# One pipeline for the first update, the second normalisation and the score tables of a two-layer graph network

## The reference, cut to what matters

```
h = max(layernorm(x), 0)
# layer 0: messages by edge type, summed by destination, then a GRU update
m = segment_sum((A[type] @ h)[src], dst);  x = x + GRU0(m, h)
h = max(layernorm(x), 0)                   # the second normalisation
# layer 1: attention over the edges of each source
score = w2 . relu(W_src h[src] + W_attr attr + W_dst h[dst] + b)
msg = segment_sum(softmax_by_src(score) * lin(h[dst]), src);  x = x + GRU1(h, msg)
```

## Time and profile before

| what | us |
|---|---|
| median of three runs (lowest, highest) | 7402.01 (7397.92, 7403.58) |
| time of the profiled execution | 7396.92 |
| its span | 7395.1 |
| layer-0 update, first turn to last add | 2476.0 to 2595.2 |
| second normalisation | 2595.2 to 2634.7 |
| score tables, first turn to last split | 2636.2 to 2810.0 |

### The profile page before, as it was taken

How to read it: one execution, slowest core, us unless ns; L and a number is a source line. 1 busy time by engine, 2 the same in 40 slices (tenths; PEclk the granted TensorE clock), 3 DMA queues, 4 the chain that set the end, 5 groups by cost and what they waited for, 6 DMA issues and landing times.

```text
span 7395.1 us, 188373 instructions
## 1 busy us (share of the span) xinstructions
PE 5695.5 (77%) x35043; PEld 4674.5 (63%) x35044; DVE 4531.8 (61%) x20027; ACT 2116.9 (29%) x6104; POOL 4910.9 (66%) x10199
## 2 busy tenths in 40 slices
PE   4555778888655747888788898886888888888885
PEld 2355555555555536777677787775677677767773
DVE  3466777777333663333333333333999999999997
ACT  3111100000000212222222222222555555555553
POOL 0377777777777105777777777776677777777771
PEclk8755555555555767656765656656888988898889
DMA  6233333333333123333333333333333333333332
GB/s 211 80 57 58 59 56 58 58 58 58 59 58 58 25 97 97 107 109 106 103 102 102 102 102 102 102 102 127 94 94 94 93 94 94 94 93 94 94 91 71
DMA packets 1128085, 648.93 MB, mean 88 GB/s; under 512 B 782034, under 2 KB 1031684, under 8 KB 1127045
## 3 DMA queue, kind: packets, MB, share of 16 engines
q1 hardware_dynamic: 766708, 357.79, 19.9%
q0 software_dynamic: 137728, 233.30, 11.2%
q10 hardware_dynamic: 223584, 57.12, 3.3%
HBM read 360.62 MB, written 311.42 MB: 91 GB/s over the span
## 4 chain that ended last, share of the span: by engine, by line
PE 26%; issue 21%; POOL 17%; DMA 15%; DVE 14%; ACT 4%; DVEq 1%; POOLq 1%; ACTq 1%; SPq 0%
DMA wide<-msg_table,ring 10%; PE banks L1278 9%; POOL wide L746 7%; PE banks L1280 6%; POOL rows_by_src L770 3%; PE banks L1325 3%; DVE h L1809 2%; DVE ring L1820 2%; DMA rows_by_src<-ring 2%; PE banks L1279 2%; DVE h L1814 2%; PE banks L1266 1%; PE banks L1190 1%; PE banks L1316 1%; ACT ring L981 1%
## 5 line engine op out<-in xcount | busy, mean ns | idle before, releaser
L770 POOL DMA_INDIRECT rows_by_src<-ring x1760 | 1784.6, 1014 | 564.7 <-issue 492.8
L746 POOL DMA_INDIRECT wide<-msg_table,ring x1664 | 1619.0, 973 | 769.3 <-issue 467.2
L1278 PE MATMUL banks<-wide,ring 128*128 x3520 | 1253.1, 454 | 238.6 <-ACT ring L974 154.0
L1278 PEld LDWEIGHTS banks<-wide,ring 128*128 128x128 f32 x3520 | 828.2, 290 | 321.0 <-issue 319.2
L1280 PE MATMUL banks<-h,ring 128*128 x3520 | 973.5, 374 | 0.0
L1280 PEld LDWEIGHTS banks<-h,ring 128*128 128x128 f32 x3520 | 845.6, 295 | 125.4
L981 ACT COPY ring<-banks 128x416 f32<-128x416 f32 x880 | 402.2, 509 | 1635.7 <-PE banks L1280 1635.7
L1190 PE MATMUL banks<-wide,ring 128*128 x3520 | 810.9, 411 | 65.9 <-DVE ring L1668 61.4
L1190 PEld LDWEIGHTS banks<-wide,ring 128*128 128x128 f32 x3520 | 780.0, 322 | 127.3 <-issue 123.5
L1777 DVE COPY ring<-ring 128x4 f32<-128x4 f32 x440 | 80.4, 183 | 1230.9 <-DMA rows_by_src<-ring 1230.8
L1155 PE MATMUL banks<-ident,ring 128*128 128x128 f32 x1248 | 424.2, 469 | 532.3 <-ACT ring L917 273.8
(11 more groups left out here) (315 smaller groups left out, 10848.6 us busy)
## 6 DMA issues: line engine op xcount, KB each, us to landing
h<-rows_by_src SPq DMA_DIRECT2D x1776, 105.0 KB, 2.0
ring<-attr_turned SPq DMA_DIRECT2D x440, 128.0 KB, 2.4
attr_turned<-ring ACTq DMA_DIRECT2D x416, 96.0 KB
rows_by_src<-ring POOLq DMA_INDIRECT x1760
wide<-msg_table,ring POOLq DMA_INDIRECT x1664
msg_table<-ring SPq DMA_DIRECT2D x100, 256.0 KB, 2.0
ring<-attr_by_dst SPq DMA_DIRECT2D x208, 64.0 KB
attr_turned<-ring ACTq DMA_DIRECT2D x208, 64.0 KB
```

The lines of the kernel that those rows point to most:

```text
L746: g.indirect_dma_start(out=A_g[:, b * GV + u, :], out_offset=None, in_=table[:, :], in_offset=bass.IndirectOffsetOnAxis(ap=A_idx[:, s, u:u ...
L770: g.indirect_dma_start(out=rows_d[:, :], out_offset=bass.IndirectOffsetOnAxis(ap=B_pos[:, s, u:u + 1], axis=0), in_=B_row[:, s, u, :], in_ ...
L1278: mm(b[:, 0:H1], B_DT[:, t, u, :], q_tab[:, w, :].rearrange("p a k -> p (a k)"), start=True, stop=False)
```

## The change

The three stages become one written-out sequence of 63 slots (`G_SLOTS` = 50 + 11 + 2) on PE, ACT, DVE, and 66 on SP. Slot k of the sequence holds, in each engine's order:

- PE: turn pair k; gate products of pair k-1; turn `h` of pair k-11 (into one bank, 4, straight from `h`, no GpSimd copy); one product of 288 columns per window for pair k-12 (banks 5 and 6, one buffer).
- ACT: copy of pair k; candidate tanh of pair k-2; gate tanh of pair k-1; in every fifth slot a `Square` of ten windows of `h`; copy to `P_hT` of pair k-11; copies of both products of pair k-12, to `q_tab` and to `P_raw` in SBUF. The copies of the edge ids (`recs1`) stand in slot 51.
- DVE: mix of pair k-1; candidate of pair k; a step of the normalisation of ten windows; the bf16 split of pair k-13, out of `P_raw`.
- SP: load of pair k's half of `h0m`; store of `P_hT` of pair k-14; store of the bf16 parts of pair k-16. The 3,200 KB stores of `xs` and `h`, the padding rows and the loads for `rows` come after the last of these.

The normalisation goes by groups of ten windows (five pairs), the steps at slots 5g+6 (sum, deviation), 5g+7 (`Square` on ACT), 5g+8 (sum of squares, then an inverse square root by shift, subtraction and three Newton rounds) and 5g+9 (one instruction for maximum and scale). ScalarE's `Sqrt` of this normalisation is gone. `normalise`, still used for the first one, loses its two multiplications by 1/64 and does maximum and scale in one instruction. VectorE's memsets of the padding buffers come after the whole sequence. The semaphores of the layer-1 update are shared with those of layer 0.

```diff
+G_GROUP = 5
+N_GROUPS = NW // 2 // G_GROUP
+G_NORM = (G_GROUP + 1, G_GROUP + 2, G_GROUP + 3, G_GROUP + 4)
+G_LAG = 2 * G_GROUP + 1
+G_SLOTS = NW // 2 + G_LAG + 2
+G_STORE = G_LAG + 5
...
@@ SP @@
+            for k in range(NW // 2 + G_STORE):
+                if k < NW // 2:
+                    if k >= H_SLOTS:
+                        sp.wait_ge(g_mm, k - H_SLOTS + 1)
+                    sp.dma_start(h0m[0:HID, k % H_SLOTS, :, :]..., h0T_d[:, k * 2 * P:(k + 1) * 2 * P])...
+                j = k - G_LAG - 3
+                if 0 <= j < NW // 2:
+                    sp.wait_ge(p_Tc, j + 1)
+                    sp.dma_start(hT_d[...], P_hT[j % 2]...).then_inc(t_keep[j % 2], 16)
+                j = k - G_STORE
+                if j >= 0:
+                    sp.wait_ge(p_p, j + 1)
+                    sp.dma_start(p_d[...], P_out[:, j % 2, ...]...).then_inc(p_st[j % 2], 16)
+            for b in range(2):
+                sp.wait_ge(t_keep[b], 16 * (T_PAIRS + G_LOOPS))
+            sp.wait_ge(g_x, NW // 2)
             sp.dma_start(xs_d[:, :], wide[:, 0:NW * HID]).then_inc(kept, 16)
-            sp.wait_ge(s_h, 3)
+            sp.wait_ge(s_h, 2 + N_GROUPS)
             sp.dma_start(h_d[:, :], h[:, :, :].rearrange("p w k -> p (w k)")).then_inc(kept, 16)
...
-            loop(sp, G_LOOPS, store_p)
...
-            loop(pool, G_LOOPS, copy_h2)
...
@@ ACT @@
+            for k in range(G_SLOTS):
+                if k < T:
+                    act.wait_ge(g_T, k + 1)
...
+                    a.copy(h0m[HID:P, k % H_SLOTS, :, :], two(bank[k % 2], P)[HID:P]).then_inc(g_Tc, 1)
+                if 2 <= k < T + 2:
+                    act.wait_ge(g_v, k - 1)
+                    a.activation(G_n[:, k % 2, :, :], G_v[:, k % 2, :, :], ACT.Tanh).then_inc(g_n, 1)
+                if 1 <= k < T + 1:
...
+                    a.activation(G_t[...], ..., ACT.Tanh, scale=0.5).then_inc(g_t, 1)
+                if k == T + 1:
+                    act.wait_ge(r_pos, R_STEP * RANK_LOOPS)
+                    a.copy(recs1[:, :, 0], src_T).then_inc(r_c, 1)
+                    a.copy(recs1[:, :, 1], place_T).then_inc(r_c, 1)
+                    act.wait_ge(r_c, 2 * REC0)
+                g, step = divmod(k - G_NORM[1], G_GROUP)
+                if 0 <= g < N_GROUPS and step == 0:
+                    act.wait_ge(s_dev, g + 1)
...
+                    a.activation(G_sq[:, g % 2, :, :], h[:, 2 * g * G_GROUP:2 * (g + 1) * G_GROUP, :], ACT.Square)...
+                j = k - G_LAG
+                if 0 <= j < T:
+                    act.wait_ge(p_T, j + 1)
+                    if j >= 2:
+                        act.wait_ge(p_mm, j - 1)
+                        act.wait_ge(t_keep[j % 2], 16 * (T_PAIRS + j // 2))
+                    a.copy(P_hT[j % 2][0:HID, :, :], two(bank[4], P)[0:HID]).then_inc(p_Tc, 1)
+                j = k - G_LAG - 1
+                if 0 <= j < T:
+                    act.wait_ge(p_mm, j + 1)
...
+                    a.copy(q_tab[:, 2 * j:2 * j + 2, :], by_window(5)[:, :, H1:2 * H1]).then_inc(p_q, 1)
+                    a.copy(P_raw[:, j % 2, :, :], by_window(5)[:, :, 0:H1]).then_inc(p_raw, 1)
...
@@ PE, behind turn k and products k-1 @@
+                j = k - G_LAG
+                if 0 <= j < T:
+                    pe.wait_ge(s_h, 2 + j // G_GROUP + 1)
+                    if j >= 1:
+                        pe.wait_ge(p_Tc, j)
+                    for u in range(2):
+                        last = tr(bank[4][0:HID, u * P:(u + 1) * P], h[:, 2 * j + u, :], ident[:, :])
+                    last.then_inc(p_T, 1)
+                j = k - G_LAG - 1
+                if 0 <= j < T:
+                    pe.wait_ge(p_Tc, j + 1)
+                    if j >= 1:
+                        pe.wait_ge(p_raw, j)
+                    for u in range(2):
+                        last = mm(bank[5 + u][:, 0:2 * H1], P_hT[j % 2][:, u, :], wab[:, :], start=True, stop=True)
+                    last.then_inc(p_mm, 1)
...
@@ DVE @@
+            def norm_group(g, step):
...
+                if step == 0:
+                    ch.link(v.tensor_reduce(total, xs[:, w, :], AX.X, ALU.add))
+                    v.scalar_tensor_tensor(h[:, w, :], per_row(total, n), -1.0 / HID, xs[:, w, :], ...).then_inc(s_dev, 1)
+                if step == 2:
+                    dve.wait_ge(s_sq, g + 1)
+                    v.tensor_reduce(var, G_sq[:, g % 2, :, :], AX.X, ALU.add).then_inc(s_var, 1)
+                    dve.wait_ge(s_var, 2 + g + 1)
+                    ch.link(v.tensor_scalar(var, var, 1.0 / HID, EPS, ALU.mult, ALU.add))
+                    ch.link(v.tensor_scalar(std.bitcast(i32), var.bitcast(i32), 1, None, ALU.arith_shift_right))
+                    ch.link(v.tensor_scalar(std.bitcast(i32), std.bitcast(i32), -1.0, float(RSQRT_BITS), ALU.mult, ALU.add))
+                    for turn_no in range(3):
+                        ch.link(v.scalar_tensor_tensor(total, std, -0.5, var, ALU.mult, ALU.mult))
+                        ch.link(v.tensor_tensor(total, total, std, ALU.mult))
+                        m = v.scalar_tensor_tensor(std, total, 1.5, std, ALU.add, ALU.mult)
...
+                if step == 3:
+                    dve.wait_ge(s_std, 2 + g + 1)
+                    v.scalar_tensor_tensor(h[:, w, :], h[:, w, :], 0.0, per_row(std, n), ALU.max, ALU.mult).then_inc(s_h, 1)
...
+                j = k - G_LAG - 2
+                if 0 <= j < T:
...
+                    ch.link(v.tensor_copy(po[0], P_raw[:, t, :, :]))
+                    ch.link(v.tensor_tensor(P_rest, P_raw[:, t, :, :], po[0], ALU.subtract))
+                    ch.link(v.tensor_copy(po[1], P_rest))
+                    v.tensor_tensor(po[2], P_rest, po[1], ALU.subtract).then_inc(p_p, 1)
```

More of the change, by code:

```diff
@@ L598, in _ @@
                 sp.wait_ge(t_keep[b], 32 * (T_PAIRS // 2))
[L600 to L606, removed]
@@ L862, in std @@
                 act.wait_ge(s_var, k)
-                a.activation(small[:, NW + w.start:NW + w.stop], small[:, w], ACT.Sqrt, bias=eps_t[:, :]).then_inc(s_std, 1)
+                a.activation(small[:, NW + w.start:NW + w.stop], small[:, w], ACT.Sqrt, bias=eps_t[:, :], scale=1.0 / HID).then_inc(s_std, 1)
             def copy_plane(k):
@@ L927, in _ @@
             pick(None, AT_LOOPS - 1)
[L930 to L964, removed]
@@ L1211, in _ @@
             pe.wait_ge(w_back, 16 * (1 + PARTS))
-            def update0(k, stages):
-                if 0 in stages:
+            T = NW // 2
+            pe.wait_ge(p_ones, 2)
+            for k in range(G_SLOTS):
+                if k < T:
                     if k >= 2:
@@ L1718, in mix @@
                 ch.link(v.scalar_tensor_tensor(G_d[:, t % 2, :, :], G_e[:, t % 2, :, :], 0.5, G_n[:, t % 2, :, :], ALU.mult, ALU.add))
-            def update0(i, s, stages):
-                if 1 in stages:
-                    t, j = stages[1]
-                    w = ds((j * G_PAIRS + t) * 2, 2)
-                    mix(j, t, h[:, w, :], g_n)
-                    v.tensor_tensor(xs[:, w, :], xs[:, w, :], G_d[:, t % 2, :, :], ALU.add).then_inc(g_x, 1)
-                if 0 in stages:
-                    candidate(i, s, two(bank[2 + s % 2], 4 * HID), g_t, g_v)
@@ new lines, in _ @@
+            T = NW // 2
+            for k in range(G_SLOTS):
+                if 1 <= k < T + 1:
+                    j = k - 1
+                    w = slice(2 * j, 2 * j + 2)
+                    mix(j // G_PAIRS, j % G_PAIRS, h[:, w, :], g_n)
+                    v.tensor_tensor(xs[:, w, :], xs[:, w, :], G_d[:, j % 2, :, :], ALU.add).then_inc(g_x, 1)
+                if k < T:
+                    candidate(k // G_PAIRS, k % G_PAIRS, two(bank[2 + k % 2], 4 * HID), g_t, g_v)
+                for step, lag in enumerate(G_NORM):
+                    g, rest = divmod(k - lag, G_GROUP)
+                    if 0 <= g < N_GROUPS and rest == 0:
+                        if step == 0:
+                            dve.wait_ge(g_x, (g + 1) * G_GROUP)
+                        norm_group(g, step)
+                j = k - G_LAG - 2
+                if 0 <= j < T:
+                    t = j % 2
+                    po = [P_out[:, t, :, i, :] for i in range(PARTS)]
+                    dve.wait_ge(p_raw, j + 1)
+                    if j >= 1:
+                        dve.wait_ge(p_p, j)
+                    if j >= 2:
+                        dve.wait_ge(p_st[t], 16 * (j // 2))
+                    ch.link(v.tensor_copy(po[0], P_raw[:, t, :, :]))
+                    ch.link(v.tensor_tensor(P_rest, P_raw[:, t, :, :], po[0], ALU.subtract))
+                    ch.link(v.tensor_copy(po[1], P_rest))
+                    v.tensor_tensor(po[2], P_rest, po[1], ALU.subtract).then_inc(p_p, 1)
```

174 lines of the change are left out of this document (76 added, 98 removed).

## The result

| | median us | lowest to highest | runs |
|---|---|---|---|
| before | 7401.66 | 7397.92 to 7408.93 | 8 |
| after | 7372.38 | 7369.21 to 7382.72 | 8 |

What follows compares the result with a forecast made beforehand. No engine bounds the three stages, which run one after the other in 334.0 us. Pipeline -70.0, moved stores +12.4, first normalisation -2.6 make -60.2: 7336.7 by the profiled execution, plus 3, forecast 7340, range 7308 to 7370.

Steps and rivals of the forecast that it cites:

- A new wait: Pipeline slot after normalisation step 0: ScalarE's `Square` and copies delay the tanh, so VectorE stalls 1.2 us once a group.
- the term for slots 13 to 49: Pipeline slots holding update, split and normalisation: 180.1 us, including seven stalls of 1.2 us, 8.4 in all.
- The parts up to slot 12: Pipeline start: memset 0.5, first candidate 3.9, first mix 1.0, slots 1 to 5 10.9, slots 6 to 12 24.5 us.
- The split: VectorE's bf16 split of a table pair, now read from SBUF: 1.60 us a pair, beside 1.79 for the update.
- The stall after a `Square`: VectorE's mix waits for ScalarE's tanh behind `Square`: 1.2 us a group, seven stalls or 8.4 us counted.
- the rival of the tables: Tanh and `Square` need different activation tables, two loads a group: +26 us, 7366; chance 0.06.
- Slots 50 to 62: Pipeline end, a ring of product, two copies and semaphores over single banks: thirteen slots at 2.7 us, 35.1.
- Extra waits 3 and clock 5: Allowances in the pipeline's length: 3 us for extra waits of written-out code, 5 us for stretches below full clock.
- The moved stores: Between last split and `rows`: loads queue behind the two 3,200 KB stores, 19.7 us to first product, 12.4 given back.
- The rival of hidden stores: The 3,200 KB stores are hidden or the loads for `rows` pass them: 7328; chance 0.11.
- The ring through SP: Slots paced by split, SP's issues and a slow `P_hT` store landing: +110 us, 7450 at 10 us landing; chance 0.03.
- The first normalisation: Its second part loses a VectorE instruction for which TensorE idled: 2.6 us gained, bounds 0 and 2.8.

Runs made afterwards that it cites:

- e1: The changed kernel with four `P_raw` buffers instead of two, so ScalarE's copies wait for a split two pairs older; 7315.21 us, ratio to before 0.9893.
- e4: The changed kernel with four `P_raw` buffers, the 3,200 KB stores behind the first four `rows` loads, and `Square` one slot later; 7290.61 us, ratio 0.9860.
- e5: The kernel before with only `normalise` changed: no multiplications by 1/64, maximum and scale in one instruction; 7395.45 us, ratio 0.9993.
- e6: e4 with GpSimd's 50 copies of `h` put back, their output unused; 7292.35 us, ratio to before 0.9855.
- e8: e1 with the two 3,200 KB stores issued by ScalarE behind its last copy, on its own queue; 7322.06 us, ratio to before 0.9897.

## Why the prediction was wrong

**The step that failed: "A new wait"**, and with it the term for slots 13 to 49. It took ScalarE's copies as work that ScalarE has room for and found one stall, behind the `Square`. It passed over the wait ahead of them, for the split of two pairs earlier, and so what is queued behind it: the tanh for the next mix waited with them in every slot and not only behind the `Square`. Measured: 222.5 us against 180.1, a miss of 42.4. e1, which moves nothing but this wait, takes 170.3. None of the named rivals came, and none of the signs of being wrong named this wait; it falls under the 0.03 for something else.

**The other terms of the stage**, which e1 shows without the wait:
- The parts up to slot 12: 42.3 us in e1 and 41.8 in after, 40.8 predicted. No stall behind a `Square` was counted for slots 6 to 12; without it e4 has 37.2.
- The split: a slot with nothing else takes 3.26, not 3.39; the term was too high by 0.13 * 37 = 4.8. A group of the normalisation adds 22.7 - 5 * 3.26 = 6.4 with its stall, not 6.0 + 1.2, 5.6 less in seven groups. The two make up, within 0.6, the 9.8 by which e1's slots 13 to 49 are below 180.1.
- A small instruction: 170 ns, started every 0.205; 0.20 predicted. A pass of 640 elements 0.81 to 0.82; 0.83 predicted.
- The stall after a `Square`: 0.91 by e4, the 1.2 was near; VectorE waits 6.8 us for the tanh in slots 13 to 49 of e1, 8.4 predicted. No `ACT_TABLE_LOAD` stands at it (737 ns for 640 elements; the estimate was 0.75), so the rival of the tables falls.
- Slots 50 to 62: 29.8 for 35.1. The ring of product and two copies is there, at 2.09 us a slot (L964 starts at 2756.31, 2758.40 and 2760.49) and not 2.7. VectorE, left two pairs behind by the last group, catches up with a split every 1.86 and waits 0.45 for the copy only at the last one.
- Extra waits 3 and clock 5: not needed. TensorE got 0.84, not "near 1.00", yet it didn't bound a slot (busy 120.2 of 170.2 us in slots 13 to 49 of e1); that rival falls too.

Against 264.0 this makes 242.2 without the wait, and 264.0 + 42.4 + 1.0 - 5.3 - 8 = 294.1 with it. The errors on the high side hid part of the miss.

**The moved stores** were right in mechanism and size: 12.4 forecast, 13.4 measured, the landings 9.8 and 17.6 behind the last split where 9.6 and 17 were worked out. By the Trainium skill's page "DMA: Bandwidth & Descriptors" (Queues, rings and completion order) each DMA engine takes the descriptors of a ring in ring order, so the loads come behind the stores; the 14.3 us to landing of the loads agree. The rival of hidden stores falls. The ring through SP never came: in after ScalarE's copy to `P_hT` never waits for its store; in e4, where the slots are shortest, it waits 8.1 us in the whole stage.

**The first normalisation:** the 2.6 us are found in e5 at their place (2.75), but what is left of them at the first turn of `acc` can't be told: before's one trace has 2476.0, and the nine with the shorter normalisation, the same up to there, 2465.9 to 2475.0. That spread of 9 us is more than the term.

**The sum.** Forecast -60.2 by the profiled execution, measured -27.3. Of the 32.9 between, 30.1 lie in the stage, 1.0 in the stores, 1.7 ahead of the first turn, 0.1 in all that follows, where +8.7, -10.2 and +1.6, none of them forecast, happen to cancel. Without the wait (e1: 7315, or 7322 by its 79.8 below before) the forecast of 7340 would have missed on the other side by 18 to 25 us and still held in the range.

## What to carry to other kernels

Ahead of work added to an engine's program, list its waits too, those for a free buffer above all, and for each what stands behind it in the engine's order: two buffers between ScalarE and VectorE tied two loops together that each had time to spare, and two more gave 52 us of the stage. ScalarE was busy 38% of the stage (112 of 294 us) and paced it. Here the large stores without a deadline belonged behind the next stage's first loads (13.8 us); on another queue they held up other transfers as much.

## What was not expected of the hardware

- A scatter by GpSimd (`DMA_INDIRECT`) takes 973 or 984 to 985 ns (median of 1,760), by whether a loop of 50 copies stands in GpSimd's program ahead of it; without it, `rows` is 9 us (before and after) and 15 us (e6 and e4) longer, attention 10 and 14 shorter. How the loop does that wasn't settled.
- `rows` and attention trade: their sum is 4358 to 4373 us in all ten kernels, while `rows` alone goes from 2308.5 to 2331.7 and attention from 2058.1 to 2028.4.
- With the 3,200 KB stores in another queue under way, two 216 KB stores landed 10.4 and 17.3 us after their issue (e8), 1.9 without them; VectorE stood 8.83 us for the first.
